# Two residual convolution blocks on one core: z_normed ahead of tanh, attend ahead of project, and a lot's group sums behind the second block's first products

## The chip, the cores and the metric

The kernel runs on one NeuronCore of one Trainium2 chip. The metric is the device time of one execution in microseconds. The engines are TensorE (PE, with its weight loads as PEld), VectorE (DVE), ScalarE (ACT), GpSimd (POOL) and SyncE (SP, which only issues DMAs here). Each has its own list of instructions and works through it in order; they meet at semaphores.

## What is computed

x is 16 images of 128 channels and 16 x 16 positions, in float32. Two blocks follow each other, each with a residual:

```
x = x + L0(group_norm(x))
x = x + L1(group_norm(x))

L0(f): h = chan_ln(f)
       q, k, v = depthwise3x3(w1 @ h)          # 8 heads of 16 channels
       q = softmax(q, channels of a head) * scale;  k = softmax(k, positions)
       ctx = k^T v;  out = silu(q ctx)
       return chan_ln(out_w @ out)
L1(f): qkv = w_qkv @ f;  y = pointwise(depthwise5x5(qkv))
       relu attention over qkv and over y, heads of 8, divided by its sums
       return batch_norm(w_proj @ both)
```

group_norm takes 32 groups of 4 channels within one image; chan_ln normalizes over the channels of each position.

## The kernel before

The images are handled as 8 pairs; a pair is one bank of 512 columns (4 tiles of 128). The program is written engine by engine with hand-placed semaphores. Its stages: group norm, layer norm, the products and the 3x3 convolution of block 0 (up to about 104 us); block 0's attention with block 1's first half behind it (104 to 211 us); block 1's convolution, and its second attention with the output.

The change is in the middle stage. All engines run the same loop there, `for step in range(FRONT1 + PAIRS + ...)` with FRONT1 = 11, and in each step work for different pairs in an order that is written out by hand. Before the change, with the pair in brackets and s for the step:

- PE: z_transpose(s-6), project(s-4), attend(s-3), context(s-2), k_back(s-1), kq_transpose(s).
- ACT: tanh(s-3), q_out(s-1), z_normed(s-5), k_out(s-1), k_exp(s).
- DVE: statistics of project(s-4)'s result with x1(s-6) inside (`moments`), silu(s-3), ctx_mask(s-2), x1_stats(s-6), k_max(s).
- POOL: mask_v, and `layernorm` (the twelve small instructions that make the scale and bias of z_normed) for pair s-4.

One pair goes through them so: kq_transpose brings k and q channel-major, k_max and k_exp make the softmax of k (lines 946 and 622), q_out and k_out copy out of PSUM (629, 635), context makes k^T v, ctx_mask scales and masks it (966, 971), attend applies it to q, tanh (641) and silu (980) follow, project multiplies by out_w, moments (859 to 872) and POOL's layernorm (403 to 416) give the statistics, z_normed (531) normalizes, z_transpose turns back, x1 (986) adds the residual, x1_stats (992) begins block 1's group norm. The semaphores named in the code that matter: project waits for `s_sl` (silu of its pair); attend for `s_cm` (ctx_mask), `s_qc` and the silu of the pair before, since they share bank 4; moments for `s_pr` (project); silu for `s_th` (tanh); z_normed for `s_ln` (POOL).

Block 1's group norm goes in three lots, by the table `GN1`: pairs 0 to 1, 2 to 4 and 5 to 7. For each lot DVE aggregates (line 833), PE sums over the group with a product of `mean4` (gn_of_block1(lot, 0)), DVE corrects the variance (gn_variance, 841 to 844), PE sums again (gn_of_block1(lot, 1)), and DVE makes scale and bias (gn_scale, 848, 773 to 783, 850). Lot index 1's sums stand in step 11. In step 11 PE also begins block 1: qkv1(0), 64 small products. DVE turns its result into the convolution's input (conv_in, 877), behind gn_scale and moments in its own list.

`product` (line 1116) and `transposes` (1112) are helpers: nearly all of PE's work has one of these two lines, and is told apart by its tiles (`owt` is project, `rings,ctxm` with 256 columns attend, `gmv,mean` a group sum, `w1t` qkv1).

Of the kernel before, what the change touches and what calls it, by code (L numbers as in the profile page):

```python
# [33 lines left out]
PAIRS = B // 2  # L34
# [29 lines left out]
GN1 = ((0, 2, 8), (2, 5, 10), (5, 8, 13))  # L64
# [12 lines left out]
def conv_blocks_kernel(nc, x, g_norm, q_w1, q_dw, k_w1, k_dw, v_w1, v_dw, out_w, g_out,  # L77
                       w_qkv, w_dw, w_pw, w_proj, bn_gamma, bn_beta, bn_mean, bn_var, out):
    ctx = ExitStack()
    with ctx:  # L80
# [418 lines left out]
        def _(act):  # L499
# [27 lines left out]
            def normed(n, src, dst):  # L527

                act.wait_ge(s_ln, n + 1)
                for xl in range(XL):  # L530
                    last = a.activation(tile(dst, xl), tile(src, xl), ACT.Identity,  # L531
                                        scale=ln_s[:, n % 2, xl:xl + 1], bias=ln_b[:, n % 2, xl:xl + 1])
                last.then_inc(s_nrm, 1)
# [82 lines left out]
            def k_exp(i):  # L616
                act.wait_ge(s_kn, i + 1)
                if i >= 2:
                    act.wait_ge(s_kt, i - 1)
                for b in range(2):  # L620
                    n = 2 * i + b
                    last = a.activation(image(ring_a[:, i % 2, :], b), image(bank[0][:, :], b), ACT.Exp,
                                        bias=kneg[:, n:n + 1], accum_out=ksum[:, n:n + 1])
                last.then_inc(s_ke, 1)

            def q_out(i):
                if i >= 2:
                    act.wait_ge(s_o, i - 1)
                a.copy(ring_b[:, i % 2, :], bank[1][:, :]).then_inc(s_qc, 1)

            def k_out(i):
                act.wait_ge(s_kt, i + 1)
                if i >= 2:
                    act.wait_ge(s_cx, i - 1)
                a.copy(ring_c[:, i % 2, :], bank[2][:, :]).then_inc(s_kp, 1)

            def tanh(i):
                act.wait_ge(s_o, i + 1)
                if i >= 2:
                    act.wait_ge(s_pr, i - 1)  # L640
                a.activation(ring_d[:, i % 2, :], bank[4][:, :], ACT.Tanh, scale=0.5).then_inc(s_th, 1)

            def z_normed(i):
                if i >= 2:
                    act.wait_ge(s_zt, i - 1)
                normed(PAIRS + i, bank[5 + i % 2][:, :], ring_e[:, i % 2, :])
# [46 lines left out]
            def half_out(i):  # L693
                act.wait_ge(s_ot, i + 1)
                a.copy(half0[:, i, :], bank[7][:, :]).then_inc(s_half, 1)

            for step in range(FRONT1 + PAIRS + 4):
                if 0 <= step - 3 < PAIRS:
                    tanh(step - 3)
                if 0 <= step - 1 < PAIRS:  # L700
                    q_out(step - 1)
                if 0 <= step - 5 < PAIRS:
                    z_normed(step - 5)
                if 0 <= step - 1 < PAIRS:
                    k_out(step - 1)
                if step < PAIRS:
                    k_exp(step)
                n = step - FRONT1
                if 0 <= n + 1 < PAIRS:
                    xg1(n + 1)  # L710
                if 0 <= n - 4 < PAIRS:
                    half_out(n - 4)
                if 0 <= n < PAIRS:
                    front1(n)
                    raw_q_out(n)
                if n == PAIRS - 1:
                    last_odd_quads(1)
                if 0 <= n - 4 < TSLOTS:
                    edges(NS + n - 4, K1)
                if n == PAIRS + 1:  # L720
                    for k in range(2):
                        edges(NS + TSLOTS + k, K1)
# [384 lines left out]
        def _(pe):  # L1107
# [179 lines left out]
            def attend(i):  # L1287
                pe.wait_ge(s_cm, i + 1)
                pe.wait_ge(s_qc, i + 1)
                if i >= 1:  # L1290
                    pe.wait_ge(s_sl, i)
                for b in range(2):
                    last = product(image(bank[4][:, :], b), ctxm[:, i % 2, b, 0:C], image(ring_b[:, i % 2, :], b))
                last.then_inc(s_o, 1)
# [16 lines left out]
            def qkv1(i):  # L1311
                pe.wait_ge(s_xg1, i + 1)
                if i == 0:
                    pe.wait_ge(s_ke, PAIRS)
                    pe.wait_ge(s_qc, PAIRS)
                    pe.wait_ge(s_kp, PAIRS)
                    pe.wait_ge(s_cm, PAIRS)
                for n in range(2):
                    if i >= 1:
                        pe.wait_ge(s_vr, 2 * i - 1 + n)  # L1320
                    units(n, ring_a[:, i % 2, :], w1t, 0).then_inc(s_qkv, 1)
# [63 lines left out]
            def gn_of_block1(c, k):  # L1385
                i0, i1, _ = GN1[c]
                if k == 0:
                    pe.wait_ge((s_ke, s_sl, s_x1)[c], PAIRS)
                gn_mean(2 + c, k, 2 * i0, 2 * (i1 - i0), gn_sums[c])

            for step in range(FRONT1 + PAIRS + 2):
                n = step - FRONT1
                if 0 <= step - 6 < PAIRS:
                    z_transpose(step - 6)
                if step == GN1[1][2] + 1:
                    gn_of_block1(1, 0)
                if 0 <= step - 4 < PAIRS:
                    project(step - 4)
                if step == GN1[1][2] + 1:
                    gn_of_block1(1, 1)  # L1400
                if 0 <= step - 3 < PAIRS:
                    attend(step - 3)
                if 0 <= step - 2 < PAIRS:
                    context(step - 2)
                if 0 <= step - 1 < PAIRS:
                    k_back(step - 1)
                if 1 <= step < PAIRS:
                    kq_transpose(step)
                if step == GN1[0][2]:
                    gn_of_block1(0, 0)  # L1410
                if step == GN1[0][2] + 1:
                    gn_of_block1(0, 1)
                if 0 <= n < PAIRS:
                    qkv1(n)
                if step == GN1[2][2] + 1:
                    gn_of_block1(2, 1)
                if 0 <= n - 1 < PAIRS:
                    kv_product(n - 1)
                if 0 <= n < PAIRS:
                    raw_q(n)  # L1420
                if step == GN1[2][2]:
                    gn_of_block1(2, 0)
                if PAIRS <= n < PAIRS + SETS_AHEAD:
                    if n == PAIRS:
                        pe.wait_ge(s_vr, 2 * PAIRS)
                    conv_two_sets(n - PAIRS)
                if n == 3:
                    attend1(n - 1)
                if 0 <= n - 3 < PAIRS:
                    o_transpose(n - 3)  # L1430
                if 0 <= n - 1 < PAIRS and n != 3:
                    attend1(n - 1)
# [63 lines left out]
```

## Time and profile before

| | |
|---|---|
| median of 3 runs | 307.2 us (306.92, 307.2, 308.47) |
| the profiled execution | 307.83 us, span 306.1 us |
| PE busy | 250.9 us (82%) |
| weight loads (PEld) | 189.8 us (62%) |
| DVE busy | 218.8 us (71%) |
| ACT busy | 151.7 us (50%) |
| POOL busy | 109.6 us (36%) |

The busy time of an engine is a mean over stages; what a change in one stage is worth depends on the engine and the wait that end last in that stage. The timeline gives start and length of each instruction, merged where equal ones follow each other; the start of an instruction can lie before the end of the one ahead of it, since they are pipelined. A wait is put down to the event that came last. "Granted clock" is the share of TensorE's 2.4 GHz that it was given: 1.00 or 0.50 (1.2 GHz).

### The profile page before, as it was taken

How to read it: one execution, taken by the hardware profiler on the slowest of the kernel's cores; microseconds unless marked ns; L12 is line 12 of the kernel's file. 1: busy time of each engine (PE TensorE's matmuls, PEld its weight loads, DVE VectorE, ACT ScalarE, POOL GpSimd, SP SyncE). 2: the span in 40 equal slices, each digit the busy share in tenths (PEclk: the TensorE clock that was granted, in tenths of full speed). 3: DMA queues.
4: the chain of work that ended last, by engine and by line, in shares of the span. 5: the costliest groups of instructions: out<-in, count | busy, mean ns of one | idle time of the engine just before them, and what ended most of it. 6: DMA issues, size and time to landing. Idle time of an engine off the chain costs nothing. (4 is left out here: it accounts for less than half of the span.)

```text
span 306.1 us, 12488 instructions
## 1 busy us (share of the span) xinstructions
PE 250.9 (82%) x5275; PEld 189.8 (62%) x5275; DVE 218.8 (71%) x684; ACT 151.7 (50%) x388; POOL 109.6 (36%) x311
## 2 busy tenths in 40 slices
PE   0249699729889779896499879997989999889995
PEld 0236477527658558675357657776779877566771
DVE  2788887605989438799876976662678888856674
ACT  0357685326994266765438345542243337822320
POOL 8036456003949334774424222211112221343100
PEclk9999799978999999999879999999999999999999
DMA  7820059991000200000002654448000000002212
GB/s 226 137 50 0 3 130 216 216 233 41 4 4 4 66 2 3 4 2 0 1 2 62 151 124 87 124 90 206 4 4 4 4 2 4 2 4 71 71 53 86
DMA packets 15496, 19.13 MB, mean 63 GB/s; under 512 B 3904, under 2 KB 9024, under 8 KB 15440
## 3 DMA queue, kind: packets, MB, share of 16 engines
q1 hardware_dynamic: 11936, 17.15, 23.4%
q10 hardware_dynamic: 3504, 1.18, 2.2%
q8 instruction: 42, 0.69, 1.0%
q14 instruction: 14, 0.11, 0.1%
HBM read 3.54 MB, written 2.20 MB: 19 GB/s over the span
## 5 line engine op out<-in xcount | busy, mean ns | idle before, releaser
L1116 PE MATMUL bank<-cin,tband 64*32 64x240 f32 (+5 forms) x2632 | 82.6, 403 | 7.7 <-DMA cin<-cin 5.5
L1116 PEld LDWEIGHTS bank<-cin,tband 64*32 64x32 f32 x2632 | 64.1, 108 | 25.1 <-issue 7.7
L579 ACT ACTIVATE tband<-tband,row_edge 128x96 f32<-128x96 f32 (+1 forms) x96 | 31.8, 398 | 33.4 <-POOL tband L428 32.5
L1112 PE MATMUL bank<-ident,rings 128*128 128x128 f32 x192 | 32.2, 297 | 18.5 <-ACT rings L531 7.5
L928 DVE STREAM_TRANSPOSE cpos<-bank 64x256 f32<-64x256 f32 x88 | 39.4, 447 | 5.4 <-PE bank L1116 4.2
L1112 PEld LDWEIGHTS bank<-ident,rings 128*128 128x128 f32 x192 | 22.7, 150 | 32.2 <-ACT rings L531 9.9
L877 DVE STREAM_TRANSPOSE cin<-bank 128x768 f32<-128x768 f32 x32 | 31.0, 975 | 8.4 <-PE bank L1116 8.4
L464 POOL TENSOR_SCALAR ring_v<-cpos,mask_b 128x512 f32<-128x512 f32 x30 | 20.9, 708 | 33.9 <-PE bank L1116 20.4
L531 ACT ACTIVATE rings<-bank,ln_b,ln_s 128x128 f32<-128x128 f32 x64 | 24.2, 464 | 13.3 <-POOL ln_b L416 13.2
L931 DVE STREAM_TRANSPOSE cpos<-bank 128x256 f32<-128x256 f32 x52 | 19.2, 418 | 14.6 <-PE bank L1116 14.5
L1116 PE MATMUL bank<-w0t,rings 128*32 128x192 f32 x512 | 24.9, 352 | 2.4 <-DVE cin L877 1.7
L428 POOL TENSOR_TENSOR tband<-taps,pw 128x160 f32<-128x160 f32 x24 | 10.6, 461 | 39.8 <-PE bank L1116 39.8
L1116 PE MATMUL bank<-w1t,rings 128*32 128x192 f32 x512 | 23.7, 339 | 1.1 <-ACT rings L671 1.1
L464 POOL TENSOR_SCALAR ring_v<-rings,mask_b 128x512 f32<-128x512 f32 x16 | 10.9, 694 | 33.5 <-ACT rings L671 33.4
L1116 PEld LDWEIGHTS bank<-w0t,rings 128*32 128x32 f32 x512 | 17.5, 118 | 8.6 <-ACT rings L554 2.8
L1116 PEld LDWEIGHTS bank<-w1t,rings 128*32 128x32 f32 x512 | 16.6, 114 | 6.3 <-issue 1.6
L1019 DVE TENSOR_SCALAR den<-bank 128x64 f32<-128x64 f32 x16 | 3.6, 224 | 23.5 <-PE bank L1116 20.6
L1116 PE MATMUL bank<-ctxm,rings 128*128 128x144 f32 x128 | 18.5, 288 | 1.1 <-DVE ctxm L1007 0.9
L1116 PEld LDWEIGHTS bank<-ctxm,rings 128*128 128x128 f32 x128 | 16.7, 190 | 2.3 <-DVE ctxm L1007 2.3
L1116 PE MATMUL bank<-gmv,mean 128*128 128x8 f32 (+2 forms) x20 | 4.5, 299 | 15.7 <-DVE gmv L833 14.8
L859 DVE BATCH_NORM_STATS2 lstats<-bank 128x6 f32<-128x128 f32 x64 | 14.6, 282 | 3.6 <-PE bank L1116 2.7
L428 POOL TENSOR_TENSOR tband<-taps,mask_c 128x96 f32<-128x96 f32 x24 | 8.1, 351 | 24.3 <-PE bank L1116 24.3
(133 smaller groups left out, 430.8 us busy)
## 6 DMA issues: line engine op xcount, KB each, us to landing
cin<-cin SPq DMA_DIRECT2D x48, 192.0 KB, 4.4
cin<-cin SPq DMA_DIRECT2D x20, 128.0 KB, 3.7
xin<-in_x_dram SPq DMA_DIRECT2D x4, 512.0 KB, 6.3
out_dram<-rings SPq DMA_DIRECT2D x16, 128.0 KB, 1.7
cin<-cin ACTq DMA_DIRECT2D x4, 128.0 KB, 3.9
taps<-tap_rows SPq DMA_DIRECT2D x16, 30.0 KB
taps<-tap_rows SPq DMA_DIRECT2D x16, 18.0 KB
rings<-in_L_conv_w_qkv_dram ACTq DMA_DIRECT2D x1, 192.0 KB, 6.7
```

What stands on the lines that cost most here:

```text
L428: g.tensor_tensor(out=dst.rearrange("p k (x o) -> p k x o", o=CG), in0=src[:, :, 0:XL].unsqueeze(3).broadcast_to([P, ks, XL, CG]), in1=wei ...
L464: last = g.tensor_scalar(ring_v[:, i % 2, b, :, 0:QC], values, mask_b[:, b:b + 1], 1.0, ALU.mult, ALU.mult)
L531: last = a.activation(tile(dst, xl), tile(src, xl), ACT.Identity, scale=ln_s[:, n % 2, xl:xl + 1], bias=ln_b[:, n % 2, xl:xl + 1])
L579: last = a.activation(dst[:, :, 1 + e], dst[:, :, 0], ACT.Copy, scale=row_edge[:, e:e + 1])
L859: return v.bn_stats(lstats[:, xl, :], tile(src, xl))
L877: v.transpose(cin[:, :, 2 * n, i // 2, :, o:o + QN // 2], ps[:, :, 0:UC].rearrange("p l (s c) -> p s l c", c=CG)).then_inc(s_cin, 1)
L928: last = v.transpose(to[half(x), :, :, g * CG:(g + 1) * CG], frm[half(n % 2), x * B * HH:(x + 1) * B * HH])
L931: last = v.transpose(to[:, :, :, g * CG:(g + 1) * CG], frm[:, 0:B * HH])
L1019: link(v.tensor_scalar(den[:, s], sums, ATT_EPS, None, ALU.add))
L1112: last = t_.transpose(tile(dst, xl), src(xl), ident[:, :])
L1116: return t_.matmul(dst, stationary, moving, start=start, stop=stop, skip_group_check=True)
```

## The change

Three orders change, one on ACT and two on PE; DVE, POOL and SP keep theirs, and no instruction is added or left out.

```diff
             for step in range(FRONT1 + PAIRS + 4):
+                if 0 <= step - 5 < PAIRS:
+                    z_normed(step - 5)
                 if 0 <= step - 3 < PAIRS:
                     tanh(step - 3)
                 if 0 <= step - 1 < PAIRS:
                     q_out(step - 1)
-                if 0 <= step - 5 < PAIRS:
-                    z_normed(step - 5)
                 if 0 <= step - 1 < PAIRS:
                     k_out(step - 1)
...
                 n = step - FRONT1
                 if 0 <= step - 6 < PAIRS:
                     z_transpose(step - 6)
-                if step == GN1[1][2] + 1:
-                    gn_of_block1(1, 0)
+                if 0 <= step - 3 < PAIRS:
+                    attend(step - 3)
                 if 0 <= step - 4 < PAIRS:
                     project(step - 4)
-                if step == GN1[1][2] + 1:
-                    gn_of_block1(1, 1)
-                if 0 <= step - 3 < PAIRS:
-                    attend(step - 3)
                 if 0 <= step - 2 < PAIRS:
                     context(step - 2)
...
                 if 0 <= n < PAIRS:
                     qkv1(n)
+                if step == GN1[1][2] + 1:
+                    for k in range(2):
+                        gn_of_block1(1, k)
                 if step == GN1[2][2] + 1:
                     gn_of_block1(2, 1)
```

ACT, one step of the attention (here the second that has a z_normed): L641 is tanh, L629 q_out, L531 z_normed, L635 k_out, L622 k_exp. Before:

```order
L622 ACTIVATE rings,ksum<-bank,kneg 128x256 x2
L641 ACTIVATE rings<-bank 128x512
L629 COPY rings<-bank 128x512
L531 ACTIVATE rings<-bank,ln_b,ln_s 128x128 x4
L635 COPY rings<-bank 128x512
```

and in the change:

```order
L622 ACTIVATE rings,ksum<-bank,kneg 128x256 x2
L531 ACTIVATE rings<-bank,ln_b,ln_s 128x128 x4
L641 ACTIVATE rings<-bank 128x512
L629 COPY rings<-bank 128x512
L635 COPY rings<-bank 128x512
```

z_normed has moved from behind tanh and q_out to between the k_exp of the step before and tanh.

PE, one step of the attention: z_transpose (`ident,rings`), project (`owt`), attend (`rings,ctxm`), context (`ring_v`), k_back. Before:

```order
L1112 MATMUL bank<-ident,rings 128x128 x4
L1116 MATMUL bank<-owt,rings 128x128 x4
L1116 MATMUL bank<-rings,ctxm 128x256 x2
L1116 MATMUL bank<-ring_v,rings 32x64 x16
L1112 MATMUL bank<-ident,rings 128x128 x4
```

and in the change:

```order
L1112 MATMUL bank<-ident,rings 128x128 x4
L1116 MATMUL bank<-rings,ctxm 128x256 x2
L1116 MATMUL bank<-owt,rings 128x128 x4
L1116 MATMUL bank<-ring_v,rings 32x64 x16
L1112 MATMUL bank<-ident,rings 128x128 x4
```

Attend and project have changed places.

PE, steps 10 and 11: from project(6) and attend(7) to the first product of raw q (`w1q`). Before:

```order
L1116 MATMUL bank<-owt,rings 128x128 x4
L1116 MATMUL bank<-rings,ctxm 128x256 x2
L1112 MATMUL bank<-ident,rings 128x128 x4
L1116 MATMUL bank<-gmv,mean 128x6
L1116 MATMUL bank<-owt,rings 128x128 x4
L1116 MATMUL bank<-gmv,mean 128x6
L1116 MATMUL bank<-w1t,rings 32x192 x32
L1116 MATMUL bank<-rings,w1q 128x512
```

and in the change:

```order
L1116 MATMUL bank<-rings,ctxm 128x256 x2
L1116 MATMUL bank<-owt,rings 128x128 x4
L1112 MATMUL bank<-ident,rings 128x128 x4
L1116 MATMUL bank<-owt,rings 128x128 x4
L1116 MATMUL bank<-w1t,rings 32x192 x32
L1116 MATMUL bank<-gmv,mean 128x6 x2
L1116 MATMUL bank<-rings,w1q 128x512
```

The two group sums of lot index 1 have moved from around project(7) to behind qkv1(0).

## Rows read from the trace of the kernel before

**Rows 1.** Timeline, DVE, one step: start us, us, engine, line, operation, tiles [idle before].
```profile
126.11 0.89 DVE L859 BATCH_NORM_STATS2 lstats<-bank 128x6 f32<-128x128 f32 x4 [1.52 <-PE bank L1116]
...
127.57 0.37 DVE L869 BATCH_NORM_AGGREGATE lmv<-lstats 128x2 f32<-128x6 f32 x4
127.98 0.54 DVE L871 TENSOR_SCALAR lnw<-lmv 128x4 f32<-128x4 f32 x1
...
128.49 0.67 DVE L980 SCALAR_TENSOR_TENSOR rings<-rings,bank 128x512 f32<-128x512 f32 x1
...
129.28 0.61 DVE L971 SCALAR_TENSOR_TENSOR ctxm<-bank,krec,mask 128x128 f32<-128x128 f32 x2
...
130.46 0.67 DVE L946 TENSOR_REDUCE kneg<-bank 128x2 f32<-128x512 f32 x1
...
131.14 0.89 DVE L859 BATCH_NORM_STATS2 lstats<-bank 128x6 f32<-128x128 f32 x4
```

**Rows 2.** Timeline, PE, the step that meets it.
```profile
129.48 0.66 PE L1112 MATMUL bank<-ident,rings 128*128 128x128 f32 x4 [0.25 <-ACT rings L531]
...
129.98 1.06 PE L1116 MATMUL bank<-owt,rings 128*128 128x128 f32 x8
...
130.87 1.07 PE L1116 MATMUL bank<-rings,ctxm 128*128 128x256 f32 x4
...
131.87 0.66 PE L1116 MATMUL bank<-ring_v,rings 128*32 128x64 f32 x32
```

**Rows 3.** Timeline, ACT, from k_exp to z_normed.
```profile
131.17 0.49 ACT L622 ACTIVATE rings<-bank,kneg 128x256 f32<-128x256 f32 x1 [1.26 <-DVE kneg L946]
...
132.09 0.60 ACT L641 ACTIVATE rings<-bank 128x512 f32<-128x512 f32 x1
...
132.57 0.59 ACT L629 COPY rings<-bank 128x512 f32<-128x512 f32 x1
...
133.03 1.54 ACT L531 ACTIVATE rings<-bank,ln_b,ln_s 128x128 f32<-128x128 f32 x4
```

**Rows 4.** Waits, 120 to 200 us: us in total, times, longest.
```profile
PE bank L1112 <- ACT rings L531: 5.9, 6, 2.1
```

**Rows 5.** Timeline, PE, attend(1) and attend(7).
```profile
116.35 1.07 PE L1116 MATMUL bank<-rings,ctxm 128*128 128x256 f32 x4
...
145.81 1.07 PE L1116 MATMUL bank<-rings,ctxm 128*128 128x256 f32 x4
```

**Rows 6.** Timeline, DVE, end of step 10 and step 11.
```profile
149.75 0.68 DVE L980 SCALAR_TENSOR_TENSOR rings<-rings,bank 128x512 f32<-128x512 f32 x1
...
151.13 0.51 DVE L833 BATCH_NORM_AGGREGATE gmv<-gstats 128x2 f32<-128x6 f32 x6
...
152.99 0.17 DVE L844 TENSOR_TENSOR gmv<-gmv,gtmp 128x6 f32<-128x6 f32 x1
...
154.53 0.17 DVE L848 COPY gtmp<-bank 128x6 f32<-128x6 f32 x1 [1.37 <-PE bank L1116]
...
159.12 1.83 DVE L877 STREAM_TRANSPOSE cin<-bank 128x768 f32<-128x768 f32 x2
```

**Rows 7.** Timeline, PE, step 11, and qkv1(1) of step 12.
```profile
151.79 0.57 PE L1116 MATMUL bank<-gmv,mean 128*128 128x6 f32 x2 [2.17 <-DVE gmv L833]
...
152.21 2.05 PE L1116 MATMUL bank<-owt,rings 128*128 128x128 f32 x8
...
154.42 4.03 PE L1116 MATMUL bank<-w1t,rings 128*32 128x192 f32 x64
...
160.99 2.81 PE L1116 MATMUL bank<-w1t,rings 128*32 128x192 f32 x64 [1.05 <-ACT rings L671]
```

**Rows 8.** Timeline, POOL, first and last of the twelve small instructions.
```profile
138.49 0.19 POOL L403 TENSOR_SCALAR lnt<-lnw 128x4 int32<-128x4 int32 x1 [1.09 <-DVE lnw L872]
...
141.57 0.20 POOL L416 TENSOR_TENSOR ln_b<-lnw,ln_s 128x4 f32<-128x4 f32 x1
```

**Rows 9.** Windows: length, busy us (instructions) of PE, PEld, DVE, ACT, POOL, granted clock, DMA share, GB/s.
```profile
143.30:150.13 6.83, 3.11 (x20) 2.38 (x20) 6.29 (x34) 4.19 (x11) 2.56 (x13) 1.00 0.00 0
150.13:156.96 6.83, 5.17 (x44) 4.19 (x48) 4.44 (x26) 2.53 (x6) 2.19 (x11) 0.50 0.01 4
```

## The prediction

> **What bounds the kernel now.** I read the windows first, then the timeline of each engine through block 0's attention, step by step, and last the waits. A "step" is one pass of the hand-written loop (steps 0 to 20), and "project(i)", "attend(i)" and so on are the work on pair i. On which engine does a step hang?
>
> In the middle of the attention, steps 6 to 8, it is DVE. Its chain of a step begins with the moments of project's result and ends with k_max: statistics at 126.11, aggregation at 127.57, silu at 128.49, the context mask at 129.28, k_max at 130.46, the next statistics at 131.14 [rows 1]. One instruction starts as the last ends: 5.03 us a step without a pause. PE and ACT fit round it. On PE project ends at 129.98 + 1.06 = 131.04, just before DVE asks for it at 131.14 [rows 1, 2]. Attend starts at 130.87, though its mask was ready at 129.28 + 0.61 = 129.89: it has 0.98 us in hand [rows 1, 2]. On ACT, tanh starts at 132.09 right behind k_exp (131.17), and z_normed takes 1.54 us at 133.03, behind tanh and q_out [rows 3]. So z_normed stands where nothing urgent is behind it. What is urgent is tanh, since silu on DVE waits for it.
>
> The PE waits for z_normed that invite the change exist (5.9 us in six waits [rows 4]), but in steps 6 to 8 DVE is full anyway. Six spacings from attend(1), 116.35, to attend(7), 145.81, make 29.46 us, 4.91 each [rows 5].
>
> In step 11 the group sums of lot 1 stand at the front of PE's queue. The operand is ready at 151.13 + 0.51 = 151.64, the first sum starts at 151.79, the variance is done at 153.16, and the last DVE piece of the step (scale) begins at 154.53 [rows 6, 7]. From there DVE needs 4.59 us to the first conversion of block 1, 159.12 [rows 6]; after it block 1 goes on with a fixed pattern, in which each step hangs on the one before. Nothing later is tied to the clock on the wall, so a delay of that conversion goes to the end unreduced.
>
> **The change, part by part.** The instructions are the same, each once; only three orders change, so there is no added work and no queue of SP or POOL is touched.
>
> *z_normed ahead of tanh (ACT).* Now k_exp, z_normed, tanh follow each other, and tanh's silu is on DVE's chain. The ring over one step: k_exp to the next instruction 0.92 (131.17 to 132.09); z_normed 1.4 (its 1.54 less the 0.1 by which neighbours overlap: tanh takes 0.60, the next starts after 0.48); tanh 0.60 and a handover of 0.1; silu to mask 0.79; mask to k_max 1.18; k_max 0.67 and a handover of 0.04 [rows 1, 3]. Sum 5.70. Without z_normed this ring was 4.3 and bound nothing. It counts only in steps with both (6 to 8).
> z_normed also waits for POOL's twelve small instructions, 138.49 to 141.77, 3.28 us after the moments [rows 8], and tanh now stands behind that wait as well. From the moments of pair i: 0.1 + 3.28, z_normed 1.4, tanh 0.6, 0.1, silu 0.79, mask 0.61, 0.1, attend 1.0, project 1.06, 0.1, and DVE back to the moments of pair i + 2, 2.1. That is 11.2 us for two steps, 5.6 each. In step 6 it is met for the first time: tanh(2) waits for z_normed(0), which waits for POOL.
>
> *attend ahead of project (PE).* Attend needs the mask, project only silu, 0.79 earlier. Now project stands behind both the wait for the mask and attend. The ring: mask 0.61, handover 0.1, attend to project 1.00 (130.87 to 131.87, to what then followed attend), project 1.06, handover 0.1, statistics to aggregation 1.46, aggregation to silu 0.92 (it holds an instruction stretched from 0.17 to 0.54), silu to mask 0.79 [rows 1, 2]. Sum 6.0, or 5.7 when that instruction isn't stretched. DVE waits 0.7 to 1.0 us a step for project: 0.1 + 1.00 + 1.06 + 0.1 = 2.26 us from mask end to statistics, of which DVE's own work up to k_max's end covers 1.24. In steps 4 and 5 there is no x1 on DVE, and the ring is some 0.65 shorter, 5.1.
> How close project follows attend no row shows. Bounds: 0.89, as attend follows project, to 1.00; I take 1.00, since the row is of what follows attend itself.
> The Trainium skill, "TensorE: Matmul & The Clock Gate", section "Step-by-step: what each phase is for", says that weight loads are pulled ahead of running products, while products stay in order. By it project's loads could hide under attend; with 0.7 in place of 1.00 the total below would be about 1 us less.
>
> *Sum to attend(7).* The rings share their pieces, so they do not add: the longest, 5.7, is the step. attend(1) itself comes 0.7 us sooner, since it needn't let project(0) pass. Then 5.1 + 5 x 5.7 + 0.4 (DVE's aggregation for lot 0 in step 8, an estimate from the 0.51 of lot 1 [rows 6]) = 34.0, against 29.46. So attend(7) comes 34.0 - 29.5 - 0.7 = 3.8 us late. Project(6) stood 0.89 in front of attend(7) and now stands 1.00 behind it: 3.8 + 1.9 = **5.7 us late**. DVE's step 10 waits for it, and lot 1's operand follows: 151.64 + 5.7 = 157.3.
>
> *Group sums behind the first products.* Silu(7) ended at 149.75 + 0.68 = 150.43 [rows 6], now 156.1. Project(7) then needs 1.0 and qkv1(0) 2.81 at full clock [rows 7]: PE reaches the first sum at 160.0 to 160.2, though its operand has lain ready since 157.3. From first product to scale takes 1.6 (151.79 to 153.16 less 0.27 for the product at full clock, plus 0.5 for the second sum): 161.7 against 154.53, **7.2 us late**. The early qkv1(0) buys nothing: its conversion stands behind scale on DVE.
>
> *Clock.* PE was busy 3.11 us of the stretch 143.30 to 150.13, and the next stretch, 150.13 to 156.96, was granted 0.50, the 1.2 GHz level [rows 9]. At it project took 2.05 in place of 1.06, qkv1(0) 4.03 in place of 2.81 [rows 2, 7]. With the change PE has the same work in more time just there, so the low stretch should come again, and qkv1(0) is now ahead of the sums: at least 1.2 us more, between 0 and 4.5 by where the stretch falls (project 1.0 twice, qkv1(0) 1.2 and its share in the next step). I take 1.1.
>
> Total 7.2 + 1.1 = 8.3. The profiled execution took 307.83, its span 306.1; it becomes 316.1. That execution is 0.6 above the median of 307.2, so **315.5 us**.
>
> **Rivals.** A measurement of this kernel can tell about 0.5% (1.5 us) from no change.
> 1. *Faster.* z_transpose waits for z_normed six times, up to 2.1 us at once, 5.9 us in all [rows 4], and DVE has pauses from step 9 on. If z_normed in front removes them, and if the ring with attend does not form (attend's 0.98 us in hand would have to cover it), step 9 on gains some 3 us: 304. It decides if DVE's moments do not wait for project. Against it: project ends 0.1 before DVE asks for it [rows 1, 2], so any delay shows. Chance 0.04.
> 2. *No change.* Gains at steps 9 to 11 cancel the longer steps: 307. 0.03.
> 3. *Slower by the end alone.* The rings stay hidden under DVE's 5.03, for instance because project follows attend closely and masks come sooner; then project(6) is 1.9 late, and the sums add 1.4: 310.5. 0.13.
> 4. *Low clock longer.* It covers project(6) to the second block's second products: 7.2 + 4.5 = 11.7, so 319. 0.20.
> My forecast has 0.60.
>
> **Range and chances.** Left out are rivals 1 and 2 and part of 3, and little above 4: 311 to 319.5. Faster 0.04, same 0.03, slower 0.93.
>
> **What would show it.** In the profile after: DVE in steps 6 to 8 waits 0.5 to 1.0 us for PE (project) before its statistics, and its period is 5.6 to 6.0; tanh follows z_normed directly; attend(7) starts 3 to 5 us later than 145.81; DVE waits some 3 us for PE before the copy of the group sum, and the first conversion of block 1 comes 7 to 10 us after 159.12; from there to the end nothing is lost or won. The prediction is wrong if steps 6 to 8 keep their 5.0 to 5.2 us, or if the first conversion comes before 163.

## The result, and the profile after

The changed kernel takes 318.73 us (median of four executions, 316.0 to 320.22), the kernel before 307.63 beside it: the ratio is **1.034, with a 95% interval of 1.028 to 1.041**, slower. The forecast was 315.5 with a range of 311 to 319.5.

The kernel before was executed 51 more times beside the experiments; the median of these is 308.8 and their mean 309.1 (305.7 to 311.9). Medians in this document are over all executions of a kernel, while the ratios leave out five that lie over 1.5% above the fastest of their kernel: one of the kernel before (311.9), three of sums only (313.67 to 315.17) and one of the first filling of the kernel before (356.24 us, at a granted clock of 0.77).

| | before | after |
|---|---|---|
| profiled execution / span | 307.83 / 306.1 us | 319.11 / 317.3 us |
| PE busy | 250.9 us (82%) | 254.8 us (80%) |
| DVE busy | 218.8 us (71%) | 219.1 us (69%) |
| ACT busy | 151.7 us (50%) | 151.3 us (48%) |
| attend(1) to attend(7) | 29.46 us | 34.38 us |
| first k_max to block 1's first conversion | 54.38 us | 64.35 us |
| that conversion to the last one | 45.80 us | 46.29 us |

The work is the same; new are pauses, and more products at 1.2 GHz. Nearly all of the loss lies between the first k_max (104.74 before, 105.43 after, so the stages ahead account for 0.69 us) and block 1's first conversion: 64.35 - 54.38 = 9.97 us. With 0.69 ahead and 0.49 behind that is 11.15 of the 11.2 us between the spans; from the last conversion to the end the two traces agree within 0.1 us. The first k_max, before and then after:

```profile
104.74 0.69 DVE L946 TENSOR_REDUCE kneg<-bank 128x2 f32<-128x512 f32 x1 [0.19 <-PE bank L1112]
```

```profile
105.43 0.69 DVE L946 TENSOR_REDUCE kneg<-bank 128x2 f32<-128x512 f32 x1 [0.19 <-PE bank L1112]
```

The timeline of DVE after the change, the statistics that each step begins with, and one k_max, with which a step ends (start, length, instruction, idle before it):

```profile
129.74 0.89 DVE L859 BATCH_NORM_STATS2 lstats<-bank 128x6 f32<-128x128 f32 x4 [1.61 <-PE bank L1116]
...
133.73 0.67 DVE L946 TENSOR_REDUCE kneg<-bank 128x2 f32<-128x512 f32 x1
135.38 0.89 DVE L859 BATCH_NORM_STATS2 lstats<-bank 128x6 f32<-128x128 f32 x4 [0.98 <-PE bank L1116]
...
141.37 0.89 DVE L859 BATCH_NORM_STATS2 lstats<-bank 128x6 f32<-128x128 f32 x4 [0.92 <-PE bank L1116]
...
147.05 0.89 DVE L859 BATCH_NORM_STATS2 lstats<-bank 128x6 f32<-128x128 f32 x4 [0.91 <-PE bank L1116]
```

The period that was 5.03 us without a pause [rows 1] (5.17 and 5.23 in the two steps behind it) is now 5.64, 5.99 and 5.68, and each step holds 0.9 to 1.0 us in which DVE waits for project on PE.

The timeline of ACT, one step:

```profile
134.44 0.49 ACT L622 ACTIVATE rings<-bank,kneg 128x256 f32<-128x256 f32 x1 [2.21 <-DVE kneg L946]
...
135.36 1.50 ACT L531 ACTIVATE rings<-bank,ln_b,ln_s 128x128 f32<-128x128 f32 x4
136.72 0.62 ACT L641 ACTIVATE rings<-bank 128x512 f32<-128x512 f32 x1
```

Against [rows 3] tanh starts 2.28 us behind k_exp's start, not 0.92: z_normed stands between them, and q_out, which follows tanh, comes later as well. ACT is idle for 2.2 us of the step, and PE still waits for it in the next lines.

The timeline of PE: attend and project in step 7; kq_transpose, z_transpose, attend and project in step 8; and from attend(7) through step 11:

```profile
133.22 1.16 PE L1116 MATMUL bank<-rings,ctxm 128*128 128x256 f32 x4
134.22 1.05 PE L1116 MATMUL bank<-owt,rings 128*128 128x128 f32 x8
...
137.96 1.06 PE L1112 MATMUL bank<-ident,cpos 128*128 128x128 f32 x8 [1.51 <-ACT rings L629]
138.86 0.60 PE L1112 MATMUL bank<-ident,rings 128*128 128x128 f32 x4
139.30 1.07 PE L1116 MATMUL bank<-rings,ctxm 128*128 128x256 f32 x4
140.21 1.05 PE L1116 MATMUL bank<-owt,rings 128*128 128x128 f32 x8
...
150.52 1.32 PE L1116 MATMUL bank<-rings,ctxm 128*128 128x256 f32 x4 [1.15 <-DVE ctxm L971]
151.64 1.91 PE L1116 MATMUL bank<-owt,rings 128*128 128x128 f32 x8
...
158.01 2.08 PE L1116 MATMUL bank<-owt,rings 128*128 128x128 f32 x8 [1.56 <-DVE rings L980]
160.02 3.58 PE L1116 MATMUL bank<-w1t,rings 128*32 128x192 f32 x64
163.53 0.39 PE L1116 MATMUL bank<-gmv,mean 128*128 128x6 f32 x2
164.77 0.39 PE L1116 MATMUL bank<-gmv,mean 128*128 128x6 f32 x2 [0.86 <-DVE gmv L844]
168.37 2.01 PE L1116 MATMUL bank<-rings,w1q 128*128 128x512 f32 x2 [3.21 <-DVE gn_b L850]
```

The lines of step 8 show what project is late for. The mask of attend(5) was done at 138.80, and attend starts at 139.30: it has not waited for the mask. It stands behind kq_transpose, which waited 1.51 us for q_out (L629), and q_out stands behind z_normed and tanh on ACT. Step 6 looks the same (1.40 us of waiting for q_out, attend 0.50 behind its mask). In step 7 kq_transpose waits 1.07 us, and attend(4) starts 0.07 us after its mask; from step 9 on attend waits for the mask.

And DVE in step 11:

```profile
158.66 0.51 DVE L833 BATCH_NORM_AGGREGATE gmv<-gstats 128x2 f32<-128x6 f32 x6
163.95 0.17 DVE L841 COPY gtmp<-bank 128x6 f32<-128x6 f32 x1 [4.78 <-PE bank L1116]
...
165.19 0.16 DVE L848 COPY gtmp<-bank 128x6 f32<-128x6 f32 x1 [0.48 <-PE bank L1116]
...
169.78 1.83 DVE L877 STREAM_TRANSPOSE cin<-bank 128x768 f32<-128x768 f32 x2
```

The operand of the group sum is ready at 159.17, and PE is then busy with project(7), just begun at 158.01, and qkv1(0). DVE waits 4.78 us where it waited 0.75 before the change. From the second copy to the conversion it takes 4.59 us, exactly as before [rows 6]. A pause that I had not named opens on PE: the first product of raw q waits 3.21 us for gn_scale, which before was done in time: there qkv1(0), at 1.2 GHz, ended at 158.45 [rows 7], and gn_b was done at 157.66.

The windows after the change, cut where the granted clock changes (busy us of PE, PEld, DVE, ACT, POOL, granted clock):

```profile
143.30:150.13 6.83, 3.98 (x54) 3.08 (x52) 5.71 (x27) 3.04 (x8) 3.01 (x16) 1.00 0.00 0
151.40:161.64 10.24, 6.86 (x45) 5.26 (x47) 5.22 (x31) 3.93 (x10) 3.15 (x16) 0.50 0.01 2
161.64:168.46 6.82, 2.75 (x53) 1.89 (x45) 3.69 (x21) 1.71 (x4) 0.00 (x0) 1.00 0.00 0
168.46:171.87 3.41, 2.99 (x10) 1.46 (x14) 3.34 (x12) 0.87 (x3) 1.83 (x10) 0.50 0.00 0
```

The low stretch (1.2 GHz) is 10.24 us long, not 6.83 [rows 9], and a second one follows right behind that new pause.

### The profile page after: what moved, and what is told of

It is laid out like the page before. It is cut to its first block and busy times, and to the rows that moved or that the text cites. A ratio compares the mean times of both kernels' runs of the same rounds, so it can differ in the third digit from the quotient of the medians.

```text
span 317.3 us, 12488 instructions
## 1 busy us (share of the span) xinstructions
PE 254.8 (80%) x5275; PEld 192.6 (61%) x5275; DVE 219.1 (69%) x684; ACT 151.3 (48%) x388; POOL 109.3 (34%) x311
## 5 line engine op out<-in xcount | busy, mean ns | idle before, releaser
L1116 PE MATMUL bank<-cin,tband 64*32 64x240 f32 (+5 forms) x2632 | 84.5, 407 | 7.4 <-DMA cin<-cin 5.3
L1116 PEld LDWEIGHTS bank<-cin,tband 64*32 64x32 f32 x2632 | 65.1, 109 | 25.6 <-issue 9.5
L1112 PE MATMUL bank<-ident,rings 128*128 128x128 f32 x192 | 33.1, 302 | 16.3 <-ACT rings L622 3.5
L1112 PEld LDWEIGHTS bank<-ident,rings 128*128 128x128 f32 x192 | 23.5, 153 | 29.9 <-issue 11.9
L531 ACT ACTIVATE rings<-bank,ln_b,ln_s 128x128 f32<-128x128 f32 x64 | 24.1, 460 | 18.9 <-POOL ln_b L416 18.5
L1116 PE MATMUL bank<-w0t,rings 128*32 128x192 f32 x512 | 23.9, 343 | 1.8 <-DVE cin L877 1.1
L464 POOL TENSOR_SCALAR ring_v<-rings,mask_b 128x512 f32<-128x512 f32 x16 | 10.9, 693 | 34.0 <-ACT rings L671 33.9
L669 ACT ACTIVATE rings<-bank 128x256 f32<-128x256 f32 x16 | 6.2, 385 | 23.7 <-DVE cin L877 23.4
L1112 PE MATMUL bank<-ident,cpos 128*128 128x128 f32 x96 | 13.5, 277 | 4.4 <-ACT rings L629 4.4
```

The source lines that it names most:

```text
L464: last = g.tensor_scalar(ring_v[:, i % 2, b, :, 0:QC], values, mask_b[:, b:b + 1], 1.0, ALU.mult, ALU.mult)
L669: a.activation(ring_c[:, i % 2, at].rearrange("p (l c) -> p l c", l=XL), ps[:, :, HC:2 * HC], ACT.Relu)
L1112: last = t_.transpose(tile(dst, xl), src(xl), ident[:, :])
L1116: return t_.matmul(dst, stationary, moving, start=start, stop=stop, skip_group_check=True)
```

## The experiments

Two theories stood against each other. The first, the *rings*: z_normed in front of tanh and attend in front of project each close a ring through DVE that is longer than DVE's own 5.03 us, and the group sums make DVE wait behind qkv1(0). The second, the *clock*: the orders are nearly harmless, and the loss comes from TensorE at 1.2 GHz. A third, that a half-idle ACT can take z_normed anywhere, speaks of the first edit alone.

### Each edit alone

z_normed only:

```diff
+                if 0 <= step - 5 < PAIRS:
+                    z_normed(step - 5)
                 if 0 <= step - 3 < PAIRS:
                     tanh(step - 3)
                 if 0 <= step - 1 < PAIRS:
                     q_out(step - 1)
-                if 0 <= step - 5 < PAIRS:
-                    z_normed(step - 5)
```

> Of the three edits only z_normed ahead of tanh on ACT. The rings theory: the ring k_exp, z_normed, tanh, silu, mask, k_max takes 5.7 us and binds steps 6 to 8, and steps 9 and 10 wait for POOL behind z_normed; attend(7) 2.5 to 3.2 us later than in the kernel before, project(6) as much, the first conversion of block 1 and the end about 3 us later (1.7 to 3.5 by how the low clock falls). Rival, that ACT has room since it is half idle: no change. Rival, that the low clock makes most of the loss of the whole change: attend(7) unmoved, the end within 1 us.

Measured: 314.03 us against 308.81, ratio 1.017 (1.013 to 1.022). Attend(1) to attend(7) takes 34.08 us, 4.6 more than before, where 2.5 to 3.2 was expected. The rival that ACT has room is out. The size was under-rated: I had 3 us. The timeline of ACT in steps 5 and 7 of this kernel, then of DVE in step 5:

```profile
123.78 1.50 ACT L531 ACTIVATE rings<-bank,ln_b,ln_s 128x128 f32<-128x128 f32 x4 [1.37 <-POOL ln_b L416]
...
136.88 1.50 ACT L531 ACTIVATE rings<-bank,ln_b,ln_s 128x128 f32<-128x128 f32 x4 [1.07 <-POOL ln_b L416]
138.26 0.61 ACT L641 ACTIVATE rings<-bank 128x512 f32<-128x512 f32 x1
```

```profile
125.80 0.69 DVE L980 SCALAR_TENSOR_TENSOR rings<-rings,bank 128x512 f32<-128x512 f32 x1 [2.59 <-ACT rings L641]
```

Here z_normed waits for POOL, 1.37 us in step 5 and 1.07 in step 7, and holds tanh back with it: this is the second ring of the prediction, the one through POOL, and it shows where project is not late as well. It does not give an even 5.7 us: from one statistics to the next the steps take 8.46, 4.99, 6.92 and 5.58 us. In this execution the low clock also fell on 127.3 to 130.8, in the middle of the attention, and the spacing from attend(2) to attend(3) was 8.4 us, against 5.4 before. Nearly all of these 3 us are the order and not the clock: k_max(5) starts at 127.48, 10.25 us behind attend(1) where it was 7.55 before, so 2.7 us were lost when the low stretch had only just begun.

attend only, with the group sums round project(7) as before:

```diff
                 if step == GN1[1][2] + 1:
                     gn_of_block1(1, 0)
+                if 0 <= step - 3 < PAIRS:
+                    attend(step - 3)
                 if 0 <= step - 4 < PAIRS:
                     project(step - 4)
                 if step == GN1[1][2] + 1:
                     gn_of_block1(1, 1)
-                if 0 <= step - 3 < PAIRS:
-                    attend(step - 3)
```

> Only attend ahead of project on PE; the group sums stand round project(7) as before. The rings theory: the ring mask, attend, project, statistics, silu takes 5.6 to 6.0 us by itself; attend(7) 2.9 us later than before, project(6) 4.7 us later, the end 4.1 to 5.8 us later. DVE waits for PE 0.7 to 1.0 us before the statistics of each of steps 6 to 8. Rival, that only z_normed's place costs: DVE's period stays near 5.1 and the end within 1 us, apart from the 1.9 us by which project(6) stands further back.

Measured: 317.03 us, ratio 1.027 (1.022 to 1.032). The timeline of DVE, two steps:

```profile
130.17 0.89 DVE L859 BATCH_NORM_STATS2 lstats<-bank 128x6 f32<-128x128 f32 x4 [1.62 <-PE bank L1116]
...
135.80 0.89 DVE L859 BATCH_NORM_STATS2 lstats<-bank 128x6 f32<-128x128 f32 x4 [0.97 <-PE bank L1116]
```

The period is 5.63 us and the wait for PE 0.97: the ring that was worked out as 5.7 stands there by itself, with z_normed back in its old place. Attend waits 0.86 and 0.96 us for its mask in these steps, as the ring through PE says; in the whole change it does not (above). Attend(1) to attend(7) takes 35.11 us, more than in the whole change: the last spacing alone is 7.01 us, and low stretches fell on 144.7 to 148.1 and 151.5 to 154.9 in this execution. The total is above the 4.1 to 5.8 us expected; the low clock, which was longer in these executions, accounts for about 2 us of it (an estimate, below).

sums only, attend and z_normed as before:

```diff
                 if 0 <= step - 6 < PAIRS:
                     z_transpose(step - 6)
-                if step == GN1[1][2] + 1:
-                    gn_of_block1(1, 0)
                 if 0 <= step - 4 < PAIRS:
                     project(step - 4)
-                if step == GN1[1][2] + 1:
-                    gn_of_block1(1, 1)
...
                 if 0 <= n < PAIRS:
                     qkv1(n)
+                if step == GN1[1][2] + 1:
+                    for k in range(2):
+                        gn_of_block1(1, k)
```

> Only the two group sums of lot index 1 behind qkv1(0). Attend(7) and the operand of the sums stay where they were; qkv1(0) starts some 2 to 3 us earlier; DVE's copy of the second sum and the first conversion come 1.0 us later where PE has the full clock, 4.6 us later where qkv1(0) falls into the low clock. Rival (what the edit is after): qkv1(0) earlier makes the end 1 to 2 us earlier.

Measured: median 312.13 against 308.81, which is 3.3 us; the ratio is 1.0065 (1.002 to 1.011), which is 2.0 us. The rival, an earlier end, is out. The timeline of PE in step 11, then of DVE:

```profile
149.70 2.08 PE L1116 MATMUL bank<-owt,rings 128*128 128x128 f32 x8 [0.86 <-DVE rings L980]
151.70 3.33 PE L1116 MATMUL bank<-w1t,rings 128*32 128x192 f32 x64
154.96 0.39 PE L1116 MATMUL bank<-gmv,mean 128*128 128x6 f32 x2
```

```profile
150.34 0.51 DVE L833 BATCH_NORM_AGGREGATE gmv<-gstats 128x2 f32<-128x6 f32 x6
155.39 0.17 DVE L841 COPY gtmp<-bank 128x6 f32<-128x6 f32 x1 [4.54 <-PE bank L1116]
156.63 0.17 DVE L848 COPY gtmp<-bank 128x6 f32<-128x6 f32 x1 [0.48 <-PE bank L1116]
161.22 0.96 DVE L877 STREAM_TRANSPOSE cin<-bank 128x768 f32<-128x768 f32 x1
```

This trace lies 0.78 us ahead of the one before (attend(1) at 115.57). Put on one base, qkv1(0) starts 1.9 us earlier than before, and the second copy and the conversion come 2.9 us later, between the 1.0 and the 4.6 that were expected at full and at low clock; a low stretch covers 149.5 to 152.9 here. So the edit does what it says and loses: the early products have nobody who can take them, since DVE is held at the group sum.

### z_normed and attend together, the sums as before

Both of the first two diffs at once; only the group sums are back round project(7).

> The change without its third part: z_normed and attend as in the change, the group sums round project(7) as before. If the parts simply add, 3 + 4.5 = 7.5 us or more over the kernel before; if the rings share their pieces, as I say, attend(7) comes 4.2 us late as in the change (34.4 us for six spacings), and the end 5.5 to 8.2 us late, less than the sum of the two single edits, and 1.6 to 2.3 us less than the change.

Measured: 317.48 us, ratio 1.029 (1.022 to 1.036), 8.7 us above the kernel before. Attend(1) to attend(7) takes 34.40 us: the same as in the whole change (34.38). The two edits alone gave 5.2 and 8.2 us, 13.4 together; side by side they give 8.7. The rings share pieces, so their delays do not add. Taking z_normed back alone would have returned nothing (attend only, 317.03); taking attend back alone would have returned 3.5 us (z_normed only, 314.03).

### Is it tanh alone that mustn't wait?

z_normed behind tanh but in front of q_out:

```diff
                 if 0 <= step - 3 < PAIRS:
                     tanh(step - 3)
+                if 0 <= step - 5 < PAIRS:
+                    z_normed(step - 5)
                 if 0 <= step - 1 < PAIRS:
                     q_out(step - 1)
-                if 0 <= step - 5 < PAIRS:
-                    z_normed(step - 5)
```

> z_normed behind tanh but ahead of q_out; nothing else changed. The narrow form of my theory (only tanh behind z_normed costs) gives no change. The wide form (z_normed in front of anything that k_max of the next pair hangs on: q_out, kq_transpose, k_max, k_exp) gives attend(7) 2.2 us later and the end 2 to 3 us later.

Measured: 313.42 us, ratio 1.013 (1.007 to 1.019). The narrow form is out. The wide form holds in its mechanism, but was sized too low: attend(1) to attend(7) takes 33.49 us, 4.0 more than before and not 2.2, and the end is 4.6 us later and not 2 to 3. A low stretch in this trace (125.6 to 128.9) has an unmeasured share in it. Q_out feeds kq_transpose, and this the next k_max. The waits of this kernel from 110 to 145 us (us in total, times, longest), kq_transpose for q_out and k_max for kq_transpose:

```profile
PE bank L1112 <- ACT rings L629: 5.6, 4, 2.3
DVE kneg L946 <- PE bank L1112: 5.5, 5, 2.6
```

In the kernel before the same two are 0.6 us (2 times) and 2.9 us (4 times). z_normed's old place is the only one of the three tried that costs nothing.

z_normed in front of tanh only from step 9 on, where there is no k_exp:

```diff
+                if step >= 9 and 0 <= step - 5 < PAIRS:
+                    z_normed(step - 5)
                 if 0 <= step - 3 < PAIRS:
                     tanh(step - 3)
                 if 0 <= step - 1 < PAIRS:
                     q_out(step - 1)
-                if 0 <= step - 5 < PAIRS:
+                if step < 9 and 0 <= step - 5 < PAIRS:
                     z_normed(step - 5)
```

> z_normed ahead of tanh in steps 9 to 12 alone, where no k_exp and no k_max close the ring. By the rings theory nothing is lost: attend(7) within 0.3 us of its place in the kernel before, the end within 0.5 us. If a z_normed in front of tanh costs by itself in each step, 1 to 1.5 us a step: 3 us or more.

Measured: 309.37 us, ratio 1.0004 (0.997 to 1.004). Attend(1) to attend(7) takes 29.25 us, 0.2 less than before. So z_normed in front of tanh is free where the ring through k_exp and k_max is open, and gains nothing there either, although those are the very steps in which PE waited longest for it [rows 4]. The trace says why: in step 10 z_normed itself now waits 3.24 us for POOL, and z_transpose still waits 1.96 us where it waited 2.08.

### What the clock costs

Each execution reports its mean granted clock. From that, 2 x (1 - clock) x span is the time spent at 1.2 GHz. In the 51 executions of the kernel before it lies between 13 and 32 us (mean 19.6), and a straight line through them rises by **0.33 us for each us of low clock** (correlation 0.82; the executions scatter by 0.8 us about the line). The change's four executions have 23.6 us on average, attend only 26.6, z_normed with attend 26.6, z_normed only 24.8. The line is a relation between executions of one kernel; that another kernel follows the same slope is assumed where it is used below.

Then I tried to take the low clock away instead: products that nobody reads, on PE, in the pauses.

```diff
+            def filler(n):
+                for _ in range(n):
+                    product(bank[1][:, 0:256], ident[:, :], w1t[:, 0:256])
+
             for step in range(FRONT1 + PAIRS + 2):
+                if step == 9:
+                    pe.wait_ge(s_qc, PAIRS)
                 n = step - FRONT1
+                if step == 11:
+                    filler(4)
                 if 0 <= step - 6 < PAIRS:
                     z_transpose(step - 6)
+                if 9 <= step <= 11:
+                    filler(4)
                 if 0 <= step - 3 < PAIRS:
                     attend(step - 3)
+                if step == 11:
+                    filler(6)
                 if 0 <= step - 4 < PAIRS:
                     project(step - 4)
```

> The change, with products that nobody reads added on PE in its pauses of steps 9 to 11 (into bank 1, free there). They keep PE busy where the clock was lost; the orders and so the rings stay. If the low clock there is 2.5 to 3.5 us of the change's loss, as the bases of the two traces suggest, the low stretch that began at 151.4 is gone, attend(7) stays at its 34.4 us from attend(1), and the time is 2 to 3.5 us below the change's. If the clock cost nothing on the path, the time stays, or is up to 1 us longer for the added products.

Measured: 321.7 us, ratio 1.040 (1.033 to 1.046). A miss: I had sized one product at 0.25 us, and it takes 0.45. The timeline of PE in step 11:

```profile
158.02 4.48 PE L1116 MATMUL bank<-w1t,ident 128*128 128x256 f32 x20
162.34 1.05 PE L1116 MATMUL bank<-owt,rings 128*128 128x128 f32 x8
```

The filling itself is what project(7) waits for; attend(7) is late too, 35.95 us behind attend(1) and not 34.4. The same error in the kernel before, with four products in steps 9 and 10, seven ahead of z_transpose and six ahead of the group sum in step 11:

> The same filling in the kernel before: four products ahead of z_transpose in steps 9 and 10, seven in step 11, six ahead of the first group sum. Its low stretch (150.1 to 157.0) goes, and with it about 1.4 us: 305.5 to 307 where the kernel before gives 307 to 308.8. If the low clock is hidden behind DVE there: no change.

Measured: median 310.36, ratio 1.003 (0.999 to 1.007), with 6.8 to 13.7 us of low clock in nine of the ten executions in place of 13 to 32. So the low clock fell and the time did not. That the late products took what the clock gave back is likely but not shown: the one trace of this kernel is of the execution of 356.24 us.

Then with fitting numbers, in the change:

```diff
                 if step == 11:
-                    filler(4)
+                    filler(2)
                 if 0 <= step - 6 < PAIRS:
                     z_transpose(step - 6)
-                if 9 <= step <= 11:
-                    filler(4)
+                if 9 <= step <= 10:
+                    filler(2)
                 if 0 <= step - 3 < PAIRS:
                     attend(step - 3)
                 if step == 11:
-                    filler(6)
+                    filler(4)
```

> The change with the added products halved, since one takes 0.45 us and not the 0.25 that the first filling was sized by: two ahead of attend in steps 9 and 10, two ahead of z_transpose and four ahead of project(7) in step 11. They fit the pauses now, so attend(7) stays 34.4 us behind attend(1) and nothing is late for them. The change's own runs lose 0.35 us for each us of low clock and spend 23.6 us there on average; with 3.4 to 7 us less of it I expect 316 to 317.5. So even at full clock in these steps the change stays 7 us or more above the kernel before: the orders make the loss, not the clock. If the clock made it, it comes below 313.

Measured: 318.46 us, ratio 1.033 (1.027 to 1.039). The forecast of 316 to 317.5 is missed, and the time is not better, but the trace gives a clean figure: from 73 to 165 us the clock is full. The timeline of PE and then of DVE in step 11:

```profile
157.73 1.16 PE L1116 MATMUL bank<-owt,rings 128*128 128x128 f32 x8 [0.29 <-DVE rings L980]
158.82 2.81 PE L1116 MATMUL bank<-w1t,rings 128*32 128x192 f32 x64
...
166.41 2.08 PE L1116 MATMUL bank<-rings,w1q 128*128 128x512 f32 x2 [3.22 <-DVE gn_b L850]
```

```profile
161.98 0.17 DVE L841 COPY gtmp<-bank 128x6 f32<-128x6 f32 x1 [3.10 <-PE bank L1116]
...
163.22 0.17 DVE L848 COPY gtmp<-bank 128x6 f32<-128x6 f32 x1 [0.48 <-PE bank L1116]
...
167.82 1.83 DVE L877 STREAM_TRANSPOSE cin<-bank 128x768 f32<-128x768 f32 x2
```

From the first k_max (105.78) to the conversion (167.82) it takes 62.04 us, against 54.38 before: the change at full clock is **7.7 us** longer there than the kernel before with its own low stretch. The other 2.3 of its 9.97 us are the low clock, and the rows of the change bear them out: at 1.2 GHz project(6) took 1.91 us and project(7) 2.08, in place of 1.05, and qkv1(0), half in the stretch, 3.58 in place of 2.81.

The 54.38 hold a low stretch too. The last kernel of this document is the kernel before with filling, and has the full clock from 100 to 160 us. The timeline of DVE, its first k_max and its first conversion:

```profile
103.95 0.69 DVE L946 TENSOR_REDUCE kneg<-bank 128x2 f32<-128x512 f32 x1 [0.24 <-PE bank L1112]
...
157.27 1.83 DVE L877 STREAM_TRANSPOSE cin<-bank 128x768 f32<-128x768 f32 x2
```

That is 53.32 us, so the low stretch cost the kernel before 1.06 us, and with full clock on both sides the orders cost 62.04 - 53.32 = **8.7 us** (up to 0.3 of it is the filling, since attend(7) is 34.70 us behind attend(1) here and not 34.38). Of the 9.97 us that leaves 1.3 for the clock.

But behind the 3.22 us pause of raw q the clock falls all the same (165.0 to 171.9 in this trace), and the executions spend 18 to 27 us low: the low stretch has moved, not gone. The clock theory is out as the main cause, and stands as an addition of 1.3 us up to the first conversion, and probably the 0.49 us behind it.

### A version that beats both

The filling pays where the orders are good. The kernel before, with `filler` and the wait at step 9 as above, and with:

```diff
+                if 9 <= step <= 11:
+                    filler(4 if step == 11 else 2)
                 if 0 <= step - 6 < PAIRS:
                     z_transpose(step - 6)
                 if step == GN1[1][2] + 1:
+                    filler(4)
                     gn_of_block1(1, 0)
```

> The kernel before with fillings that fit its pauses: two products ahead of z_transpose in steps 9 and 10, four in step 11 and four ahead of the first group sum. Low clock falls from 20 us to 12 us or so as in the first filling, without its lateness: 306 to 307.5, 1.5 to 3 us below the kernel before. If the pauses are too short for them too, no change.

Measured: 306.96 us against 309.03, ratio 0.995 (0.992 to 0.999), with 10.9 us of low clock on average.

And with ten more while PE waits for the transfers ahead of block 0's convolution:

```diff
+            for _ in range(10):
+                product(bank[7][:, 0:256], ident[:, :], w0t[:, 0:256])
             for n in range(NS):
                 if n == 2:
                     pe.wait_ge(s_wte, 2)
                 conv(n, K0)
```

> As the kernel before with the fitted filling, and ten more products while PE waits 5.5 us for the transfers ahead of the first convolution set (into bank 7, free there), so that block 0's convolution starts at full clock: a further 1 to 1.7 us less, 304.5 to 306.5. This is the version that should beat both kernels. If the convolution's start hangs on the bands and not on PE: no gain over the other.

Measured: **305.62 us, ratio 0.991 (0.987 to 0.995)**: 0.9% faster than the kernel before, small but with the interval below 1, and 13 us faster than the change. The windows of this kernel, the middle and last over the same times as [rows 9]:

```profile
64.00:72.00 8.00, 6.72 (x179) 5.76 (x186) 2.29 (x5) 2.29 (x7) 0.96 (x3) 1.00 0.75 169
143.30:150.13 6.83, 6.26 (x36) 5.25 (x36) 6.32 (x32) 3.43 (x8) 2.85 (x15) 1.00 0.02 4
150.13:156.96 6.83, 5.90 (x83) 4.09 (x82) 5.37 (x36) 2.54 (x6) 1.84 (x10) 1.00 0.00 0
```

PE is busy 6.26 us of the stretch in which it was busy 3.11, and the stretch behind it keeps the full clock. Over its eight executions the low clock is 2.8 us on average, from 0 to 6.7. Attend(1) to attend(7) takes 29.50 us against 29.46, so the products delay nothing there. All the same the gain is smaller than the line promises: 16.8 us less of low clock would be 5.5 us, and 3.4 were measured. Where the rest goes no run shows. Not tried was a filling of the remaining pauses of block 1 in this kernel.

## Why the prediction was right, point by point

**DVE bounds steps 6 to 8.** Right: the delays of its operands showed in its period, 5.64 to 5.99 us for 5.03.

**The rings.** The number is right, the path only in part. Forecast 5.7 us a step; measured 5.64, 5.99 (the step with the aggregation) and 5.68, with 0.9 to 1.0 us of waiting for project, where 0.5 to 1.0 was forecast. Attend(1) to attend(7) was forecast as 34.0 and is 34.38 us; the whole difference lies in the first spacing, 5.55 for the 5.1 of the forecast. That the rings don't add is shown by z_normed with attend: 34.40 us and 8.7, not 13.4. But the prediction let project be late because attend waits for its mask. That holds in attend only. In steps 6 and 8 of the change attend had its mask 0.50 us before, and stood behind kq_transpose, which waited for q_out behind z_normed on ACT. The prediction did not name this path; that it is about as long as the 5.7 us of the other two is luck.

**The first z_normed.** The prediction has tanh(2) wait for z_normed(0) in step 6. By the loop both stand in step 5, and z_normed only shows there what it costs: silu(2) waits 2.59 us. This piece is missing from the sum of z_normed alone.

**attend to project.** Taken as 1.00 us with 0.89 as the other bound. Both occur: 0.91 where attend had not waited (139.30 to 140.21), 1.00 where it started as its mask came (133.22 to 134.22). The Trainium skill, "TensorE: Matmul & The Clock Gate", section "Step-by-step: what each phase is for", says that weight loads are pulled ahead of running products. The 0.7 us that the prediction takes for that case, without a working, is not seen in this trace.

**Project(6) 5.7 us late.** It starts at 151.64; less the 0.69 of the earlier stages and against 144.92 (0.89 ahead of attend(7) [rows 5]) that is 6.0.

**The group sums.** Forecast 7.2 us at full clock for the first conversion; the filled version of the change measures 7.7. DVE's wait before the first copy was forecast as some 3 us and is 3.10 at full clock, 4.78 with the low stretch. Both totals stand against a kernel before that has its low stretch; against full clock it is 8.7. The edit alone costs, qkv1(0) coming earlier for nothing.

**The clock.** This is the term that was mis-sized. "I take 1.1": the low stretch in these steps cost 2.3 us (9.97 less 7.7), since it covered project(6) and project(7) besides half of qkv1(0). What was missing from the prediction altogether was the pause of 3.2 us that raw q makes on PE by waiting for gn_scale. A second low stretch follows it (168.46 to 171.87), and the part behind the first conversion takes 0.49 us longer. I had held that nothing is lost or won there. By the straight line, 4.0 us more of low clock over all its executions (23.6 against 19.6) are 1.3 us of the 9.3 us between the means (318.4 and 309.1), which leaves 8.0 for the orders. The traces, with full clock on both sides, give 8.7 and the same 1.3.

**The base.** The forecast was made from a median of 307.2. The later executions have 308.8, which would put 1.6 us of the difference between 315.5 and 318.7 in the base; the four beside the change have 307.63, which puts only 0.4 there. By these the change costs 11.1 us (10.5 by the ratio) where 8.3 was forecast, so the forecast lies on the low side by a quarter. Which base is the right one is not settled.

**The rivals.** Faster and no change: out, with an interval of 1.028 to 1.041. Slower by the end alone (310.5): out, since the attention's steps are longer by themselves. Low clock longer (319): it gave the measured time more closely than my own forecast, and its mechanism is there: the low stretch starts at 151.40 and covers project(6), project(7) and half of qkv1(0). But it cost 2.3 us and not the 4.5 priced, so the closeness of 319 is luck.

**Single edits.** My expectations for z_normed alone (about 3) and attend alone (4.1 to 5.8) were too low; 5.2 and 8.2 were measured. By the same straight line, low clock would explain 1.7 us of the first and 2.3 of the second. That leaves attend alone near the upper bound and z_normed alone at 3.5; these are estimates from four executions each.

## What to carry to other kernels

An engine that is half idle still has an order: before moving a piece forward, close the ring through it (here k_exp, z_normed, tanh, silu, mask, k_max, and through q_out and kq_transpose as well) and compare its length with the period of the busiest engine. A visible wait (z_transpose for z_normed, 5.9 us in all) is worth nothing while another engine sets the period, or while what is waited for waits itself, as z_normed does for POOL. A small product that others wait for belongs in front of a large one whose result nobody can take yet.

Where executions of one kernel spread, plot them over their mean granted clock first. If they lie on a line, products that nobody reads, fitted to PE's pauses, can be a gain of their own, as they were in the kernel before (0.9%); in the change they gained nothing, and too long they cost as much as they give or more.

## What was unexpected in the hardware

Most of the spread of this kernel's executions, 305.7 to 311.9 us, follows the time at 1.2 GHz: with a correlation of 0.82 the line accounts for two thirds of the variance. The low stretches also fall at other places from one execution to the next. The kernel before with the fitted filling has the same instructions as the kernel before up to step 9, and its trace has a low stretch at 105.4 to 108.8, where the kernel before showed none.

The clock fell after a stretch in which PE never stood idle for more than 2.1 us at once, only often (3.11 us busy of 6.83 [rows 9]). And a product of 128 x 256 in float32 takes 0.45 us at full clock, where two attend products of that shape in 1.07 [rows 2] could have told me so: the mean of one record is not the time of one product, as each product has two.
